# An audio tower on one core: last layer's features projected unnormed through folded weights, eps beside the squares, and a new order of all slots

## What is computed

```python
norm_h = _fp32_layernorm(h, fln_g, fln_b)
out = norm_h @ proj_w + proj_b
...
h = h + _L0_attn_ref(_layernorm(h, axis=-1), L0_attn_w_qkv, L0_attn_w_proj)
h = h + _L0_ffn_ref(_layernorm(h, axis=-1), ...)
```

## Time and profile before

| | before |
|---|---|
| runs, us | 624.17, 621.41, 624.65 |
| profiled execution, us | 617.57 |
| its span, us | 615.8 |
| PE busy, us | 560.8 (91%) |
| VectorE, ScalarE, GpSimd busy, us | 319.6, 319.5, 290.7 |
| granted clock of PE, mean | 0.971 |

### The profile page before, as it was taken

One profiled execution on the slowest core, in us unless ns is written; L12 is line 12 of the kernel. 1 busy time (PEld: TensorE's weight loads), 2 busy tenths in 40 slices (PEclk: granted clock), 3 DMA queues, 4 the chain that ended last, 5 costly groups with the idle time before them and its releaser, 6 DMA issues.

```text
span 615.8 us, 11336 instructions
## 1 busy us (share of the span) xinstructions
PE 560.8 (91%) x4195; PEld 524.1 (85%) x4195; DVE 319.6 (52%) x755; ACT 319.5 (52%) x507; POOL 290.7 (47%) x425
## 2 busy tenths in 40 slices
PE   6876899999999998999999999989999877789996
PEld 6675799988988998998999889988898765689995
DVE  4654356446476665755674766555554433342222
ACT  1645467555574656557465656664553413254441
POOL 5673276876339525842864495333333120114333
PEclk9998999999999999999999999999999976699999
DMA  6290000492000000000000000000000085041210
GB/s 185 59 300 11 2 1 10 117 241 53 2 1 1 15 2 1 1 6 0 3 1 6 1 2 6 1 1 0 6 3 5 1 238 135 5 129 54 58 37 11
DMA packets 17521, 26.36 MB, mean 43 GB/s; under 512 B 2172, under 2 KB 13397, under 8 KB 17467
## 3 DMA queue, kind: packets, MB, share of 16 engines
q1 hardware_dynamic: 14155, 15.85, 9.4%
q0 software_dynamic: 3296, 9.78, 6.2%
q10 hardware_dynamic: 16, 0.00, 0.0%
HBM read 17.13 MB, written 9.18 MB: 43 GB/s over the span
## 4 chain that ended last, share of the span: by engine, by line
PE 73%; POOL 8%; ACT 7%; DVE 6%; issue 4%; DMA 1%; SPq 1%; POOLq 0%; DVEq 0%; ACTq 0%
PE ps L760 18%; PE ps L752 9%; PE ps L749 7%; PE ps L772 5%; PE ps L1015 4%; POOL rstd L595 3%; PE ps L825 3%; PE ps L846 3%; PE ps L1004 3%; PE ps L1003 3%; POOL rstd L604 2%; ACT h L1400 2%; ACT work L1371 2%; PE ps L886 2%; PE ps L816 2%
## 5 line engine op out<-in xcount | busy, mean ns | idle before, releaser
L1371 ACT ACTIVATE work<-ps 128x512 f32<-128x512 f32 (+7 forms) x128 | 67.2, 525 | 182.4 <-PE ps L754 98.1
L760 PE MATMUL ps<-wt,wide 128*128 128x128 f32 (+2 forms) x1248 | 150.5, 274 | 5.9 <-ACT wide L1389 5.8
L760 PEld LDWEIGHTS ps<-wt,wide 128*128 128x128 f32 (+2 forms) x1248 | 144.6, 184 | 9.3 <-issue 6.5
L601 POOL TENSOR_TENSOR varv<-ssum,ceps 128x4 f32<-128x4 f32 (+7 forms) x128 | 26.0, 203 | 203.2 <-DVE ssum L1090 203.0
L604 POOL TENSOR_TENSOR rstd<-varv,neghalf 128x4 f32<-128x4 f32 (+7 forms) x128 | 116.8, 913 | 10.0
L1090 DVE TENSOR_REDUCE ssum<-work 128x4 f32<-128x512 f32 (+7 forms) x128 | 75.5, 590 | 85.3 <-ACT work L1371 85.2
L1100 DVE TENSOR_TENSOR work<-ps,rstd 128x512 f32<-128x512 f32 (+7 forms) x128 | 76.3, 596 | 82.8 <-POOL rstd L604 82.7
L1389 ACT ACTIVATE wide<-ps,lncol 128x512 f32<-128x512 f32 (+6 forms) x120 | 109.2, 910 | 2.6 <-PE ps L772 1.9
L595 POOL TENSOR_TENSOR rstd<-var,half 128x10 f32<-128x10 f32 (+2 forms) x39 | 83.6, 2151 | 8.9 <-DVE var L1056 8.9
L1400 ACT ACTIVATE h<-ps,lncol 128x512 f32<-128x512 f32 (+1 forms) x120 | 81.8, 725 | 2.1 <-PE ps L825 2.1
L752 PE MATMUL ps<-wt,h 128*128 128x256 f32 x304 | 76.1, 384 | 0.0
(11 more groups left out here) (224 smaller groups left out, 839.0 us busy)
## 6 DMA issues: line engine op xcount, KB each, us to landing
sorted_tokens<-zero POOLq DMA_DIRECT2D x1, 5886.5 KB, 30.0
W2s<-in_L_ffn_W_dram SPq DMA_DIRECT2D x9, 576.0 KB, 8.3
wide<-in_L_ffn_W_dram SPq DMA_DIRECT2D x8, 576.0 KB
cols<-sorted_tokens SPq DMA_DIRECT2D x13, 96.5 KB, 1.9
xnat<-in_x_dram SPq DMA_DIRECT2D x7, 135.0 KB
wt<-in_L_ffn_b_dram SPq DMA_DIRECT2D x1, 864.0 KB, 4.5
wide<-in_L_tok_conv_w_dram SPq DMA_DIRECT2D x4, 192.0 KB, 3.4
common_sums<-acc POOLq DMA_DIRECT2D x1, 579.0 KB, 6.3
```

The source lines that it names most:

```text
L760: last = nc.tensor.matmul(y[0:rows, j * C:(j + 1) * C], h[l - 1][g % 2][:, at:at + rows], wt[:, TAP0[l] + tap, :], start=(tap == 0), stop= ...
L1371: nc.scalar.activation(sq[0:rows, n % 2, 0:w], ybank(n)[0:rows, 0:w], ACT.Square).then_inc(sq_done, 1)
```

## The change

**Projection.** The last norm's scale and offset and its centring are folded into the projection's weights once, at tile 0 (`fold_weights`, `fold`, `fold_keep`). `project` then takes the raw features h6 as they lie, channels on partitions, without a norm or a turn. The statistics of h are still made from the turned features; the reciprocal spread multiplies the projected rows in `stat_1`, in the instruction that adds the offset. norm_h, turn_norm_h and affine_h are gone for each tile.

**Eps.** The squares of a block are written with one more column that holds C * eps, and the sum over 129 columns contains it, so GpSimd's add (L601) is gone.

**Waits.** The wait for W2 moves from the first up to the first down; qkv waits for `place` where project did.

**Order.** HEAD, body, LAST and DRAIN are written anew, with other orders of chunks, products and token steps; the number of slots and the tiles' starts are the same.

```diff
+BODY = [
+    ((1, 0, 0), [('xt', 0, 2)], []),
+    ((1, 0, 1), [], []),
+    ((4, -2, 0), [('l0', 0, 2, 0)], []),
+    ((2, -1, 1), [('l0', 0, 2, 1), ('l0', 0, 2, 2)], []),
...
-        ((1, g, 0), [], []),
-        ((1, g, 1), [("xt", g, 2)], []),
-        ((4, g - 2, 0), l0(g, 2, 0, 1), []),
-        ((2, g - 1, 0), l0(g, 2, 2), []),
...
-    ((1, 0, 6), l0(1, 0, 0, 1, 2) + [("xt", 1, 1)], [("xs", 1, 1)]),
-    ((1, 1, 0), l0(1, 1, 0, 1, 2), []),
+    ((1, 0, 6), [('l0', 1, 0, 1), ('xt', 1, 1), ('l0', 1, 0, 2), ('l0', 1, 0, 0), ('l0', 1, 1, 1), ('l0', 1, 1, 0), ('l0', 1, 1, 2)], [('pow', 1, 4), ('xs', 1, 1)]),
...
-    ((6, G7, 0), [], []),
-    (None, down(3), []),
...
+    ((6, 7, 0), [], []),
+    (None, [('down', 3)], []),
+    (None, [('up', 2, 1)], []),
     (None, [], []),
-    (None, down(4), []),
-    (None, up(2, 2), []),
...
-STEP_AT = {"turn_h": 3, "stat_h": 3, "power_h": 3, "norm_h": 4, "turn_norm_h": 5, "affine_h": 5, "project": 6,
...
+RUN_1 = {'turn_h': 3, 'stat_h': 3, 'power_h': 3, 'project': 4, 'stat_1': 5, 'power_1': 4, 'norm_1': 7, 'turn_1': 8, 'copy_1': 8, 'qkv': 9, 'split_queries': 9, 'split_keys': 9, 'scores': 10, 'mask': 10, 'less_max': 10, 'exp': 10, 'sum_probs': 11, 'turn_probs': 12, 'copy_probs': 12, 'values': 13, 'divide': 13, 'turn_heads': 15, 'copy_heads': 15, 'out_project': 16, 'residual': 16, 'power_2': 16, 'norm_2': 17, 'turn_2': 18, 'copy_2': 18, 'logits': 19, 'choose': 19, 'rank': 20, 'slot': 20, 'scatter': 23}
...
+RUN_7 = {'turn_h': 3, 'stat_h': 3, 'power_h': 2, 'project': 3, 'stat_1': 3, 'power_1': 3, 'norm_1': 4, 'turn_1': 5, 'copy_1': 5, 'qkv': 5, 'split_queries': 5, 'split_keys': 5, 'scores': 7, 'mask': 7, 'less_max': 9, 'exp': 5, 'sum_probs': 9, 'turn_probs': 7, 'copy_probs': 9, 'values': 11, 'divide': 11, 'turn_heads': 12, 'copy_heads': 12, 'out_project': 12, 'residual': 11, 'power_2': 12, 'norm_2': 11, 'turn_2': 15, 'copy_2': 15, 'logits': 15, 'choose': 15, 'rank': 16, 'slot': 15, 'scatter': 12}
...
+        work = sb("work", [P, 8 * (C + 1) + 1024])
+        sq = work[:, 0:8 * (C + 1)].rearrange("p (b j c) -> p b j c", b=2, c=C + 1)
+        xh = work[:, 8 * (C + 1):].rearrange("p (b c) -> p b c", b=2)
-        varv = sb("varv", [P, 4, 4])
+        projg = sb("projg", [P, D])
...
+            gp.memset(sq[:, :, :, C:C + 1], C * EPS).then_inc(s_const, 1)
...
-                gp.tensor_tensor(varv[0:rows, idx, 0:count], ssum[0:rows, idx, 0:count], ceps[0:rows, 0:count],
-                                 ALU.add).then_inc(varv_done, 1)
-                gp.wait_ge(varv_done, n + 1)
-                gp.tensor_tensor(rstd[0:rows, idx, 0:count], varv[0:rows, idx, 0:count],
+                gp.tensor_tensor(rstd[0:rows, idx, 0:count], ssum[0:rows, idx, 0:count],
                                  neghalf[0:rows, 0:count], ALU.pow).then_inc(rstd_done, 1)
...
-                if f == 0:
-                    pe.wait_ge(s_xt, hi)
-                    pe.wait_ge(s_w2, 16 * NE)
+                pe.wait_ge(s_xt, hi)
...
+                if i == 0:
+                    pe.wait_ge(s_w2, 16 * NE)
+                pe.wait_ge(j_act, ACT_TO[max(JOB[("up", p, f)] for f in range(NF)) + 1])
                 for f in range(NF):
...
+                if step == "fold":
+                    pe.wait_ge(j_act, ACT_TO[HEAD_JOBS])
+                    pe.wait_ge(j_dve, DVE_TO[HEAD_JOBS])
+                    pe.wait_ge(t["gw"], 1)
+                    nc.tensor.matmul(pa[:, 0:D], centre[:, :], projg[:, :], start=True, stop=True).then_inc(t["fw"], 1)
+                    pe.wait_ge(t["ow"], 1)
+                    nc.tensor.matmul(pb[0:M, 0:D], act[:, 0, :], projw[:, :], start=True, stop=True).then_inc(t["fb"], 1)
                 if step == "turn_h":
                     pe.wait_ge(act_done, NUMBER[(6, r, 0)] + 1)
                     if r >= 1:
                         pe.wait_ge(t["x2"], r)
                     else:
-                        pe.wait_ge(j_act, ACT_TO[HEAD_JOBS])
-                        pe.wait_ge(j_dve, DVE_TO[HEAD_JOBS])
+                        pe.wait_ge(s_fold, 1)
                     nc.tensor.transpose(pa[0:M, 0:C], h6[:, :], ident[:, :]).then_inc(t["h6r"], 1)
-                if step == "turn_norm_h":
-                    pe.wait_ge(t["xh1"], r + 1)
-                    if r >= 1:
-                        pe.wait_ge(t["less"], r)
-                    nc.tensor.transpose(pb[:, 0:M], xn[:, 0:C], ident[0:M, 0:M]).then_inc(t["xhT"], 1)
                 if step == "project":
                     if r == 0:
-                        pe.wait_ge(s_tw, 16 * len(WEIGHTS))
-                    if r >= 1:
-                        pe.wait_ge(t["place"], r)
-                    pe.wait_ge(t["a1"], r + 1)
-                    nc.tensor.matmul(pa[0:M, 0:D], act[:, 0, :], projw[:, :], start=True, stop=True).then_inc(t["pj"], 1)
+                        pe.wait_ge(s_fold, 2)
+                    else:
+                        pe.wait_ge(t["less"], r)
+                    nc.tensor.matmul(pb[0:M, 0:D], h6[:, :], projg[:, :], start=True, stop=True).then_inc(t["pj"], 1)
                 if step == "turn_1":
                     pe.wait_ge(t["xn2"], r + 1)
                     turn2(xn, t["xn2T"])
                 if step == "qkv":
-
                     pe.wait_ge(t["a2"], r + 1)
+                    if r >= 1:
+                        pe.wait_ge(t["place"], r)
                     for j in range(4):
                         o = (pa, pb)[j // 2][0:DH, (j % 2) * M:(j % 2 + 1) * M]
                         for k in range(2):
...
-                w = count * C
                 ve.wait_ge(sq_done, n + 1)
-                nc.vector.reduce_sum(ssum[0:rows, n % 4, 0:count],
-                                     sq[0:rows, n % 2, 0:w].rearrange("p (j c) -> p j c", c=C), axis=X).then_inc(ssum_done, 1)
+                nc.vector.reduce_sum(ssum[0:rows, n % 4, 0:count], sq[0:rows, n % 2, 0:count, :], axis=X).then_inc(ssum_done, 1)
...
+                if step == "fold_weights":
+                    ve.wait_ge(s_tw, 16 * len(WEIGHTS))
+                    nc.vector.tensor_scalar(projg[:, :], projw[:, :], lncol[:, 7:8], None, ALU.mult).then_inc(t["gw"], 1)
+                    nc.vector.tensor_copy(act[:, 0, :], lncol[:, 15:16].to_broadcast([P, M])).then_inc(t["ow"], 1)
+                if step == "fold_keep":
+                    ve.wait_ge(t["fw"], 1)
+                    nc.vector.tensor_copy(projg[:, :], pa[:, 0:D]).then_inc(s_fold, 1)
+                    ve.wait_ge(t["fb"], 1)
+                    nc.vector.tensor_tensor(projb[:, :], projb[:, :], pb[0:M, 0:D], ALU.add).then_inc(s_fold, 1)
                 if step == "stat_h":
                     stat(pa[0:M, 0:C], "1", t["h6r"], r)
-                if step == "norm_h":
-                    normed(xn[:, 0:C], pa[0:M, 0:C], "1", t["xh1"], r)
                 if step == "stat_1":
+                    ve.wait_ge(t["pj"], r + 1)
+                    ve.wait_ge(t["rs1"], r + 1)
                     if r == 0:
-                        ve.wait_ge(s_tw, 16 * len(WEIGHTS))
-                    ve.wait_ge(t["pj"], r + 1)
-                    nc.vector.tensor_tensor(x1[:, :], pa[0:M, 0:D], projb[:, :], ALU.add).then_inc(t["x1"], 1)
+                        ve.wait_ge(s_fold, 2)
+                    nc.vector.scalar_tensor_tensor(out=x1[:, :], in0=pb[0:M, 0:D], scalar=rs[:, 0:1], in1=projb[:, :],
+                                                   op0=ALU.mult, op1=ALU.add).then_inc(t["x1"], 1)
                     stat(x1[:, :], "2", t["x1"], r)
                 if step == "norm_1":
                     normed(xn[:, :], x1[:, :], "2", t["xn2"], r)
...
-                nc.scalar.activation(sq[0:rows, n % 2, 0:w], ybank(n)[0:rows, 0:w], ACT.Square).then_inc(sq_done, 1)
+                nc.scalar.activation(sq[0:rows, n % 2, 0:CUTS[l][k], 0:C], ybank(n)[0:rows, 0:w].rearrange("p (j c) -> p j c", c=C),
+                                     ACT.Square).then_inc(sq_done, 1)
...
-                if step == "affine_h":
-                    ac.wait_ge(t["xhT"], r + 1)
-                    nc.scalar.activation(act[:, 0, :], pb[:, 0:M], ACT.Identity, bias=lncol[:, 15:16],
-                                         scale=lncol[:, 7:8]).then_inc(t["a1"], 1)
```

188 lines of the change are left out of this document (75 added, 113 removed), and 33 rows, old and new, of tables (BODY, HEAD).

## The result

| | before | after |
|---|---|---|
| median (lowest to highest of 4 runs), us | 623.28 (621.41 to 624.65) | 582.4 (581.28 to 584.22) |
| ratio after / before, 95% interval | | 0.9349 [0.9309, 0.9389] |
| profiled execution, us (span) | 617.57 (615.8) | 581.46 (579.7) |
| mean granted clock in it | 0.971 | 0.984 |
| PE busy, us | 560.8 | 549.2 |

The change gains 40.9 us in the medians and 36.1 us from one profiled execution to the other. The forecast was 22.7 us and 601.5 us, so the time lies 19 us under it and outside its range (591 to 614).

A forecast was written before the change was run, and what follows sets the result against it. PE's instruction stream plus about 55 us of waits was taken to bound the kernel. Head 5.2, body 4.8, last and drain 2.5 and tile 7's tokens 10.2 sum to 22.7, giving 601.5 us from 624.2; range 591 to 614.

The forecast's parts named there:

- Fold and eps: Fold's removed turns: nothing, bounds -1 to +2; GpSimd's add gone: nothing credited, bound 1.5 us.
- Head: Layer-0 batches issued earlier, so GELU waits between 44 and 75 us shrink: saving 5.2 us, bounds 2 to 9.
- Body: Exp one slot earlier in tiles 0 to 4 removes PE's wait for a GELU: saving 4.8 us, bounds -1 to 5.4.
- The opening step: Whole kernel: PE's stream hardly changes, so only its waits, about 55 us, and the low clock some leave can be won.
- Last and drain up to 493 us: Tile 5's waits for norm_h and place vanish, tile 6's exp runs under other work: saving 2.5 us, bounds 1 to 3.5.
- Tile 7's tokens: From out_project of tile 6 to rank 7, shorter chain and filled waits: saving 10.2 us; 5.0 to 16.2 by clock.
- The sum: Savings read from the profiled execution, 22.7 us in all, subtracted from the median 624.2: 601.5 us.
- rivals, 1: Clock holds to the end: gain 16.2 in the tail, 28.7 in all, 595.5 us; chance 0.12.
- Rivals 2 and 3: 2: tail at half clock, new head waits, 612, chance 0.18; 3: PE bound as before, waits just move, 623, chance 0.05.
- Rival 4: Body: exp queued early blocks ScalarE, delaying squares, norm and PE's turn; slower, 630 us at 3 us per exp; chance 0.05.
- the low gain: Lower end of the summed savings: 2 + 1 + 1 + 5 = 9 us.
- the high gain: Upper end of the summed savings: 9 + 5.4 + 3.5 + 16.2 = 34 us.

The follow-up runs named there:

- experiment 1: Kernel before with only eps moved beside the squares and GpSimd's add gone, old projection and order: 614.58 us, ratio 0.9891.
- experiment 7: Kernel after with GpSimd's add, of zero, put back ahead of each power: 591.69 us, ratio 0.9514.
- 8: Kernel after with the same GpSimd add behind each power, on constants, outside the chain: 584.02 us, ratio 0.9387.
- experiment 2: Kernel after's folded projection and eps with all rows and places of the kernel before: 607.0 us, ratio 0.9774.
- experiment 9: Kernel after with the head's rows of the kernel before, all else new: 595.35 us, ratio 0.9569.
- experiment 6: Kernel after with only the exponentials of tiles 0 to 4 one slot later, as in the kernel before: 587.16 us, ratio 0.9448.
- experiment 10: Kernel after with 20 idle transposes of a constant in TensorE's wait before turn_probs of tile 7: 582.15 us, ratio 0.9373.
- experiment 12: Kernel after with tile 7's exponentials behind two more GELUs, an up ahead of turn_probs, and idle transposes ahead of seven tile 7 steps: 584.9 us, ratio 0.9404.
- 3: Fold and eps with the new head, all other order as in the kernel before: 600.01 us, ratio 0.9636.

## Why the prediction was wrong, by its own steps

**Fold and eps: wrong, and the largest error of reasoning.** The step that failed reads "a norm that comes 0.3 us earlier saves PE's stream nothing". The 0.3 us was right (0.28). That PE rarely waits for GpSimd was right too. But VectorE does: it waits for the power 90 times in the kernel before, in its own order, and what it has queued behind comes later by each hop. And PE's brackets hid the price, most likely in modelled ends of matmuls: with eps moved PE's busy time fell by 1.6 us in four periods, its idle time by 0.2. Alone on the old order this is worth 4.4 us at equal clock (experiment 1), in the new order 7.4 by the traces and 9.3 in the medians (7), and a like add outside the chain 1.6 (8). I had bounded eps by 1.5 us, from PE's brackets; the bound should have come from the sum of hops (128 x 0.28 = 36 us) on the one side. The fold's body share (0.1 a period) was rightly nothing; its 6 us in tile 7's tokens (2) I had booked under the tail.

**Head: the right mechanism, sized at less than half.** 5.2 us forecast, 11.8 in the trace, 13.0 in experiment 9. The waits named (2.35, 2.19, 2.65, 1.39) were to give 6.2 less 1 for new waits. In fact all brackets together went from 10.8 to 1.7 us, 9.1 us: the four that I named (8.6) and three more (1.0, 0.8 and 0.4) nearly vanished, and of the two at 53.38 and 61.72, 4.84 us together, only 0.77 + 0.21 were left. What I took off for latencies and new waits was not there. The other 2.7 us are busy time, which fell as the clock's dip at 53 to 66 us went (the 1.5 that I kept for the bound).

**Body: the exponentials right, the period wrong by what eps gives.** 4.8 forecast for five tiles, 4.8 measured when this step alone was put back (6). The period fell by 1.75 us, not 0.95, with eps for 0.45 in the old order and more in the new. The opening step, that the change "can only win waits, and the low clock", fails here by the profile's account: PE's idle time fell by 0.9 us a period, and its busy time by 0.7 at full clock. The rest of the new body's share (7.3 less 4.8, the chunks' order and the other places) is not split further.

**Last and drain up to 493 us: mis-sized.** 2.5 forecast. From slot 107 on it is 5.5 us, of which 1.25 belong to tile 4's exponentials (what experiment 6 loses there), so 4.3. The wait at 487.81 is gone, as said; what eps gave there (0.8 to this point in experiment 7) is a part of the rest.

**Tile 7's tokens: right, the last part by luck.** 10.2 forecast, 10.1 measured. Turn_1 comes 8.8 us after out_project (said: 8.5), rank 7 after 31.0 (said: 31), the gap before turn_probs is 3.19 (said: near 3), down 3 fills turn_2's wait. The wait at the up before values was 0.37, not 1.3: the table load (484.82 to 486.10) ran while PE did the turns (484.86 to 486.06), and the GELU that frees the bank came right behind it, at 486.11. From the start of exp to values it takes 3.3 us instead of 2.9, a loss of 0.4; from turn_heads to turn_2 1.1 us are won where 2.3 were forecast for down 5. So two terms were about 1 us off each, in opposite ways. The clock stayed at 1.00 up to 482.9, as expected, and the half clock behind the gap was expected as well; experiment 10 adds that filling the gap gains nothing in the whole.

**The sum: wrong base.** "I subtract them from the median, as waits of fixed length should be the same in both" failed. The profiled execution of before, at clock 0.971, was one of its shorter ones. Of its 20 other runs beside the experiments 2 had 0.971 and the rest 0.953 to 0.967, and they were longer in step with it (0.971: 617.6 to 618.5 us; 0.961 to 0.963: 621.6 to 622; 0.956: 623.7 to 624.5). The kernel after had 0.978 to 0.984 in its four, and its median lies 0.9 us above its profile, not 5.7. So the medians gained 4.8 us that no row of one trace holds. That its fewer waits keep the clock up is argued, not shown: the kernel of experiment 2, with the old order and its waits, has 0.984 in three of four runs. Profile against profile, the miss is 13.4 us: head 6.6, the stretch from slot 25 to 43 1.3, body 3.2, last and drain 2.0, tail -0.1, behind it 0.3.

Of the rivals, 1 (full clock to the end) did not happen: the clock was 0.50 from 482.9 to 496.6 us and from 500.0 to 503.4. Rivals 2 and 3 are out by the time and by the head's waits, which nearly vanished. Rival 4 is out as well: no wait of PE in the body stands beside exp any more. The range was too high at its lower end because each term's upper bound was read from PE's waits, and neither the price of the hops nor the clock of the timed runs shows there. The sums had slips too: the low gain takes the body at +1, where its bound was -1, the high gain leaves out the bounds for fold and eps (2 and 1.5), and three chances that add up to 0.90 "less a small tail" aren't 0.91. None of them would have made the range wide enough.

## What to carry to other kernels

When a link is taken out of a chain that every block passes, ask which in-order engine waits for that link, and what else stands in its queue: the price is paid there, and the waits shown for the bound engine are no upper bound for it. Testing the same instruction in the chain and beside it tells latency from load in two runs. And a saving read from one profile is to be set against that profile, with the clock of the timed runs beside it: here 0.01 of mean clock went with about 4 us.

## What the runs showed that I had not expected

The granted clock is lost again after it has been saved: with 20 transposes (experiment 10) the clock of 1.00 lasted to 489.8 us instead of 482.9, and then fell. It can fall in a full stretch (experiment 12: PE busy 2.66 of 3 us at 488 to 491, 3.00 of 3 at 491 to 494). In the kernel after it fell once where PE stood idle (482.9) and once in the down after the ranks (500.0). And it can differ from one execution to the next with the same instructions, as in experiment 12 at 473.3 us. What decides it is left open here.

Three kernels (3, 7, 8) had profiled runs in which the first block of layer 1 began 2.8 to 3.0 us later than in the kernel after, with a clock of 0.92 between 8 and 52 us where the kernel after has 1.00. All of it lies ahead of that block: the clock stood at 0.50 for 6.8 us from 19 us on. Others with the same head began on time, so it isn't the order; why the clock fell there wasn't tried.
